# A 22-tile transformer block on one core: second layer norm a step later, weight splitting begun in the embedding and moved inside ScalarE's step

## The reference

```python
h = tok(x, W)                          # 64*36 tokens of 192
h = h + attn(layernorm(h), ...)        # 12 heads of 16, causal, within one image
h = h + ffn(layernorm(h), ...)         # router, best 2 of 8 experts, hidden size 768
# ffn: for each expert e:
#   out += w_e * (gelu(flat @ w1[e] + b1[e]) @ w2[e] + b2[e])
```

## Time and profile before

| | us |
|---|---|
| median of three runs | 428.76 |
| profiled execution | 429.13 |
| its span, first to last instruction | 427.0 |
| PE busy, share of the span | 356.2, 83% |
| DVE busy | 256.3, 60% |
| ACT busy | 212.6, 50% |
| POOL busy | 171.0, 40% |
| mean granted TensorE clock | 0.895 |

### The profile page before, as it was taken

One profiled execution on the slowest core, in us unless ns is written; L12 is line 12 of the kernel. 1 busy time (PEld: TensorE's weight loads), 2 busy tenths in 40 slices (PEclk: granted clock), 3 DMA queues, 4 the chain that ended last, 5 costly groups with the idle time before them and its releaser, 6 DMA issues.

```text
span 427.0 us, 14485 instructions
## 1 busy us (share of the span) xinstructions
PE 356.2 (83%) x5558; PEld 329.8 (77%) x5558; DVE 256.3 (60%) x662; ACT 212.6 (50%) x431; POOL 171.0 (40%) x214
## 2 busy tenths in 40 slices
PE   4979899989989989897522189999999999999910
PEld 4979889879979989786422179999999999999810
DVE  3787368855856877876459634555555555555426
ACT  5767576775765777663330034444444444444400
POOL 9136221253353362232630244555555555554210
PEclk9999999977977999997555569999999999999985
DMA  8982023442331233236016021323312232222058
GB/s 257 342 252 85 18 56 88 129 122 53 90 112 46 81 111 111 51 108 176 3 47 174 9 48 48 87 58 86 83 54 82 59 86 75 66 50 49 29 192 334
DMA packets 29671, 42.79 MB, mean 100 GB/s; under 512 B 12384, under 2 KB 19408, under 8 KB 29608
## 3 DMA queue, kind: packets, MB, share of 16 engines
q1 hardware_dynamic: 25480, 33.37, 25.9%
q0 software_dynamic: 4128, 8.50, 7.2%
HBM read 30.23 MB, written 9.67 MB: 93 GB/s over the span
## 4 chain that ended last, share of the span: by engine, by line
PE 37%; issue 7%; DVE 6%; POOL 4%; DMA 3%; ACT 1%; SPq 0%; POOLq 0%; DVEq 0%; ACTq 0%
PE PSA L1218 19%; PE PSA L1233 14%; DMA W2h<-yrows 2%; POOL XF L473 2%; PE PSA L1237 2%; PE PSA L1185 2%; DVE PTR L920 1%; POOL REG L480 1%; DVE H L987 1%; DMA REG<-xrows,KBR 1%; POOL REG L479 1%; DVE VB L918 1%; DMA yrows<-KBR 1%; DVE VB L914 1%; PE PSA L1117 0%
## 5 line engine op out<-in xcount | busy, mean ns | idle before, releaser
L1218 PE MATMUL PSA<-YT,W1h 128*128 128x128 f16 x774 | 79.8, 222 | 1.3 <-ACT PTR L665 0.7
L1218 PE MATMUL PSA<-YT,W1l 128*128 128x128 f16 (+1 forms) x516 | 76.9, 222 | 0.0
L1233 PE MATMUL PSA<-W2h,PTR 128*128 x516 | 70.9, 246 | 0.3 <-DVE PTR L679 0.3
L1218 PEld LDWEIGHTS PSA<-YT,W1h 128*128 x774 | 64.8, 99 | 5.4 <-DVE YT L949 1.7
L510 POOL DMA_INDIRECT yrows<-KBR x43 | 43.0, 999 | 64.1 <-DVE KBR L964 64.1
L665 ACT ACTIVATE PTR<-PSA 128x768 f32<-128x768 f32 x43 | 34.8, 810 | 64.8 <-PE PSA L1218 64.8
L1233 PE MATMUL PSA<-W2l,PTR 128*128 x258 | 63.5, 246 | 0.0
L505 POOL DMA_INDIRECT REG<-xrows,KBR x43 | 41.8, 972 | 43.3 <-DVE KBR L941 25.6
L670 ACT ACTIVATE PTR<-PTR 128x768 f16<-128x768 f32 x43 | 36.3, 844 | 44.3 <-PE PSA L1237 44.3
L679 DVE SCALAR_TENSOR_TENSOR PTR<-PTR 128x768 f16<-128x768 f32 x43 | 41.2, 958 | 27.0 <-ACT PTR L670 27.0
L1218 PEld LDWEIGHTS PSA<-YT,W1l 128*128 (+1 forms) x516 | 50.6, 98 | 0.0
(11 more groups left out here) (162 smaller groups left out, 781.6 us busy)
## 6 DMA issues: line engine op xcount, KB each, us to landing
WSTG<-w SPq DMA_DIRECT2D x16, 384.0 KB, 3.4
WSTG<-w SPq DMA_DIRECT2D x16, 336.0 KB, 3.4
REG<-xt SPq DMA_DIRECT2D x12, 324.0 KB, 5.4
W1l<-xt SPq DMA_DIRECT2D x10, 324.0 KB, 7.2
VB<-VP SPq DMA_DIRECT2D x99, 19.1 KB
H<-hrows SPq DMA_DIRECT2D x6, 288.0 KB, 2.8
xrows<-REG SPq DMA_DIRECT2D x1, 1600.5 KB
hrows<-H SPq DMA_DIRECT2D x1, 1296.0 KB
```

The source lines that it names most:

```text
L1218: ins = nc.tensor.matmul(bank(2 * u + f // (FC // 2), 128, FC // 2 * ST_)[:, w:w + ST_], weights[a, c], YT[0:rows, at:at + ST_], start=k = ...
L1233: nc.tensor.matmul(bank(4 + u, ST_, C), GP[a][:, at:at + ST_], weights[b], start=(f, a, b) == (0, 0, 0), stop=False)
```

## The change

Three edits, all in tables and orders; no instruction is added or removed.

- The second norm of tile t begins in step t+6 and not t+5, save that tiles 13 and 14 both begin in step 19 and tile 15 in step 20 (as before); the pairs from tile 16 on stay.
- Six pieces are split in the steps -6 to -1, during the embedding; from step 0 on it is one piece a step, and two in every fourth step (3, 7, 11, 15, 19); the last is in step 20. SP loads the first three pieces between patches 8 to 10 and not behind all patches.
- In ScalarE's step the first piece stands right behind the exponentials; only a second one stays at the end.

```diff
+        EARLY = 6
+
+        def pieces_upto(i):
+            return max(0, EARLY + i) if i < 0 else min(2 * PIECES, EARLY + 5 * i // 4)
+
         def pieces(i):
-            return range(max(0, 3 * i // 2), min(2 * PIECES, 3 * (i + 1) // 2))
+            return range(pieces_upto(i), pieces_upto(i + 1))
...
-            at = {t: t + 5 for t in range(NT)}
+            at = {t: t + 6 for t in range(NT)}
+            at.update({NT - 9: NT - 3, NT - 8: NT - 3, NT - 7: NT - 2})
             at.update({t: NT - 1 + (t - (NT - 6)) // 2 for t in range(NT - 6, NT)})
...
                 patches(t)
-            for n in range(WSLOTS):
-                weights(n)
+                if t - XSLOTS < WSLOTS:
+                    weights(t - XSLOTS)
             sp.wait_ge(consts_set, FILLS)
-            for i in range(-2, NT + 1):
+            for i in range(1 - EARLY, NT + 1):
...
                 if has(i):
                     exps(i)
+                for n in pieces(i)[0:1]:
+                    piece_hi(n)
                 if has(i + 3):
                     v_hi(i + 3)
...
-                for n in pieces(i):
+                for n in pieces(i)[1:]:
                     piece_hi(n)
```

## The result

The changed kernel takes **436.25 us** (median of 4 runs, 434.51 to 438.5) against 426.67 us (median of 4, 424.22 to 429.3) for the kernel before: a ratio of 1.0227, 95% interval 1.0131 to 1.0322, so slower.

What follows compares the result with a forecast made beforehand. Attention was taken as bound by TensorE. 429.13 - 16.0 (removed stalls) + 0.4 (later exponentials) + 10.3 (waits for pieces) + 10.0 (clock) + 2.0 (clock at step 20) = 435.8, so 436 us; range 425 to 445.

Steps and rivals of the forecast that it cites:

- the early pieces: Three loads ahead of patches: put at 0, between 1.5 us gained and 3.6 us of full DMA engines lost.
- the clock: Half clock behind late-piece pauses: 10.0 us for two drops, after steps 4 and 8, and 2 us at step 20.
- The removed stalls: Steps 6+7, 10+11, 14 and 18: the later norm saves 16.0 us, low clock included; 0.4 us comes back.
- the price of the two norms: Step 20: tile 13's copy must precede tile 14's transposes; counted within 3.5 us, plus 0.4 for the second copy.
- The late pieces: TensorE's waits through pieces in steps 4, 8, 12, 16 and 20: 2.6, 1.4, 1.2, 1.2, 3.5 plus 0.4; 10.3 us.
- The chain for step 4: Piece 11, from step 2's start: issued at 14.5, landed at 17.9, ScalarE free at 15.35; waits 2.55 us.
- the first rival: Pieces land at 2.9 us, waits are 7.8 us, step 8's pause does no harm: 428.3 us; chance 0.26.
- the second rival: The clock falls at steps 12 and 16 too, two more half-clock stretches: 445.8 us; chance 0.17.
- My rule for when the clock falls: TensorE pauses of 1.36 to 1.61 us in one place are followed by 1.2 GHz, one of 1.21 is not.
- my sign that the early loads cost something: Step 0 starting later than 48.42 by more than 1 us would show a cost in what was put at 0.
- The fourth: Pieces are on time, no waits or clock drops, given a landing 2.2 us sooner: 413.5 us; chance 0.07.
- The third: No clock drop before step 20, because the pauses are split in two: 425.8 us; chance 0.08.

Runs made afterwards that it cites:

- Experiment 7: Kernel before with four large overwritten matmuls in each of steps 6, 10, 14 and 18 and six in step 0; 421.30 us, ratio 0.9836.
- Experiment 1: Kernel before with only the second norm of a tile a step later; 422.10 us, ratio 0.9966.
- experiment 3: Changed kernel with the pieces put back at the end of ScalarE's step; 419.57 us, ratio 0.9851.
- experiment 5: Changed kernel with four staging slots in place of three; 421.23 us, ratio 0.9987.
- experiment 4: Changed kernel with the loads of pieces 3 to 31 issued on ScalarE's DMA queue at the end of its step, not by SP; 441.16 us, ratio 1.0404.
- experiment 2: Kernel before with only the early pieces and five pieces to four steps, at the end of ScalarE's step; 422.32 us, ratio 0.9934.
- Experiment 12: Changed kernel with four staging slots, the shared second norms a step later (tiles 14 and 15) and six large matmuls in step 0; 416.06 us, ratio 0.9853.
- experiment 10: Changed kernel with four staging slots and the two second norms that share a step moved to step 20 (tiles 14 and 15); 419.05 us, ratio 0.9888.
- experiment 6: Kernel before with eight small overwritten matmuls in each of steps 6, 10, 14 and 18; 425.26 us, ratio 0.997.
- experiment 8: Kernel of experiment 3 with twelve small overwritten matmuls in step 0; 420.02 us, ratio 0.9913.
- experiment 9: Kernel of experiment 8 with the two second norms that share a step moved one step on (tiles 14 and 15); 416.68 us, ratio 0.9878.

## Why the prediction held, point by point

**The total.** 436 us was forecast and 436.25 measured. Against its own profile the sum gave +6.7 us, and the spans differ by 8.2. Two terms that were off help each other to that (the early pieces and the clock, below), so it is luck that the total came so close, and the steps matter more than the sum. The steps are those of one execution of each kernel.

**The removed stalls**: -15.6 forecast, -16.50 measured at the same places. Experiment 7 splits the 16: 9.4 clock (10 by my figures of 5.1 and 4.8), the rest stalls. In executions of the kernel before near 420 us (mean clock 0.913, in the profiled one 0.895) most of these 9.4 us were, by that clock, not there, so this part of the gain differs from run to run. Experiment 1 shows that the norm row makes the upper half of the pause; the rest, 0.6 to 0.8 us, hangs on the two pieces ahead of the exponentials. That step 20 would get the price of the two norms was right too, but in the sum it stood under the late piece. Without any late piece it is 2.3 us (experiments 3 and 5 against the 5.1 of before).

**The late pieces.** Places, releasers and the four-step rhythm were as written. The chain for step 4 was 14.5 (issue) and 17.9 (landing) from the start of step 2. Measured: 80.62 - 65.78 = 14.84, and 84.84 - 65.78 = 19.06; ScalarE was ready at 81.24, 15.46 after (15.35 forecast). So the issue was right (experiment 4 shows the 3.0 us behind the nine) and the landing of 3.4 us was too short for this load, 4.2; the wait became 3.60 in place of 2.55. For steps 8, 12 and 16 the landing took 3.2, 3.1 and 3.1 by the chain of waits, and TensorE's pauses were 0.87, 1.32 and 0.20 in place of 1.4, 1.2 and 1.2. For step 20, 3.86 in place of 3.9. Together 9.96 us of pause in place of 10.3. The Trainium skill, "DMA: Bandwidth & Descriptors", section "Anatomy of one DMA — SWDGE (gpsimd) path", would give an estimate of 2.9 us for 384 KB; it is fitted to DMAs that GpSimd issues, and the decisive load, issued by SP, took 4.2, so here the measurement, not that line, has to be taken, and the first rival that went with it (428.3) did not come. (The landing row, 2.9 to 6.0, is that of all 32 loads and not of 16; the shortest 384 KB load took 3.0.)

**The clock.** Here the mechanism was right, the half clock behind the late pieces, but the term was mis-sized: I put 5.0 us on each of two stretches, and 2 on step 20. After step 4's piece it was 12.55 - 5.85 - 3.71 = 3.0, in step 9 9.30 - 6.17 = 3.1, in step 13 7.71 - 6.18 = 1.5 (that is half of the second rival, which saw steps 12 and 16 fall), in step 16 none, in step 20 some 1.1 (TensorE busy for 6.04 us against 4.98 at full clock in experiment 3). These 8.7 us stand against 12. A stretch at half clock does not cost a fixed sum, then; it costs by its length. Length and mean granted clock give the time at 0.50: 10.3 us in steps 6 and 7 of the kernel before (19.06 at 0.73), 6.8 in step 5 (12.55 at 0.73), 6.9 in step 9 and 3.4 in step 13. The costs, 4.7, 3.0, 3.1 and 1.5 us, are 0.44 to 0.46 of that each time. My rule for when the clock falls did not hold either: I took 1.21 us as harmless, and the half clock of step 9 followed a pause of 0.87.

**The early pieces: 0 forecast, +4.50 us measured** in steps 0 and 1, outside my bounds of -1.5 and +3.6. This step of the prediction failed. I had looked at what the loads cost while patches land, and at what ScalarE does; I had not asked whether the pause of step 0 was safe, 1.30 us in the kernel before:

```profile
52.24 0.58 PE L1068 MATMUL PSA<-IDF,PR 108*108 108x108 f32 x4 [1.30 <-ACT PR L595]
```

It became 1.76, and 4.0 of the 4.50 us are half clock in steps 0 and 1. The other 0.46 goes with the piece in front: where step 0 is not filled, the pause is 1.76 in all four profiles that have it and 1.30 in experiments 2 and 3, which have the pieces at the end. Experiment 12 shows that filling the pause takes the half clock away (12.05 us for steps 0 and 1 in place of 16.02). What the early pieces themselves have to do with it is not settled. All six profiles with early pieces and nothing in step 0 show half clock there, and none of the three without early pieces does, but in two of the six the pause is 1.30 us as before (experiments 2 and 3), and runs of the kernel of experiment 10 near 415.5 us suggest that it also goes without. The later start of step 0, by 1.34 us, was to be my sign that the early loads cost something. It was a poor sign: in the four profiles without early pieces (kernel before, experiments 1, 6 and 7) step 0 starts anywhere from 48.42 to 49.89. What the loads do cost among the patches is small: ScalarE waits 1.72 and 0.75 us for two patches at 23.1 and 24.9 us, which it does in none of those four, and TensorE waits 0.88 us from 22 to 25 us, where it waits 0.36 to 0.45 in those.

**Not in the sum:** -0.80 us in steps 2 and 4, where one piece less stands ahead of the exponentials, and +1.14 from step 21 on.

**The rivals.** The fourth, that the pieces come in time, would have been the truth with one slot more: 421.2 us in experiment 5. It asked for a landing 2.2 us sooner; a slot more asks some 9 us sooner. Its 413.5 us did not come even so, mainly for the half clock of steps 0 and 1 (some 4 us) and the two norms of step 20 (2.3 us). The third, no clock drop before step 20, fell with steps 5 and 9.

## What to carry to other kernels

An operation that is moved forward in an in-order engine brings its wait along: before moving one up, work out when its data lands, from the slot that must come free, through the queue that issues the load, to the landing, and add a slot if that is later than the new place. Where a kernel's runs spread by several microseconds, look for pauses of TensorE that are followed by a granted clock of 0.50, and give the engine real work in them before moving any code: 22 large matmuls without any use were worth 8 us of the median here. A total that comes out right is no proof of its terms: only the table by steps showed that 4.5 us in the first two steps had been missed and 3 us of clock counted too much.

## What the runs showed of the hardware

- The granted clock after a pause is not a matter of the pause's length alone. 1.30 us in step 0 was followed by 1.00 (kernel before, experiment 1) and by 0.50 (experiments 2 and 3); 0.66 us beside large matmuls by 1.00 (experiment 12), 0.44 us beside small ones by 0.50 (experiment 8); 0.87 us in step 8 by 0.50 in step 9 (changed kernel). With the same work in step 0 it differs from one execution to the next (experiments 8 and 9).
- The kernel before ran between 419.95 and 437.75 us beside these experiments; with its pauses filled by large matmuls (experiment 7) all four runs lay between 418.7 and 422.0. Its runs fall into four groups, each with a mean granted clock of its own: 420 to 421 us (0.913), 424 to 426 (0.902), 429 to 432 (0.89) and 434 to 438 (0.88). So most of its spread is TensorE's clock.
- A stretch at half clock cost 0.44 to 0.46 of the time that it lasted where TensorE was busy throughout or nearly so (3.0 us for 6.8 in step 5, 1.5 for 3.4 in step 13).
- A piece's load (336 or 384 KB) took 3.0 us at the least and 3.3 in the median in the changed kernel, and 4.2 where it mattered most; the three among the patches took 7.5 to 10.5. With two asked for within 0.4 us, the piece started 5.1 us after the first (experiment 4).
